# Attention scores of an adaLN layer: rotated q and k transposed once, their high and low rows placed by transfers

## The reference

```
mod = silu(c) @ wmod                      # six rows of 256 a batch: sa ca ga sb cb gb
h   = layernorm(x) * (1 + ca) + sa
q,k,v = h @ Wq + bq, h @ Wk + bk, h @ Wv + bv   # 16 query heads and 4 key/value heads, 16 wide
q,k = rope(q), rope(k)                    # pairs (even, odd) turned by the position's angle
y   = softmax(causal(q k^T / 4)) v        # scores of the four query heads of a key head are summed
x   = x + ga * (y @ Wo + bo)
h   = layernorm(x) * (1 + cb) + sb
x   = x + gb * ffn(h)                     # router, small linear block, rmsnorm, gated 704-wide mlp
```

## Time and profile before

| | |
|---|---|
| median of 3 runs | 486.77 us (486.62 to 486.94) |
| the profiled execution, its own time | 489.17 us |
| its span in the profile | 487.4 us |
| TensorE busy | 444.7 us, 91% |
| VectorE busy | 338.9 us, 70% |
| ScalarE busy | 281.7 us, 58% |
| GpSimd busy | 225.8 us, 46% |

### The profile page before, as it was taken

The page is one execution under the profiler, slowest core; times in us unless marked ns, Lnnn a source line. Parts: engine busy times, 40 slices in busy tenths (PEclk is TensorE's granted clock), DMA queues, the critical chain, the costliest instruction groups (busy, mean ns, idle before and its releaser), DMA issues.

```text
span 487.4 us, 9404 instructions
## 1 busy us (share of the span) xinstructions
PE 444.7 (91%) x3320; PEld 372.3 (76%) x3320; DVE 338.9 (70%) x745; ACT 281.7 (58%) x574; POOL 225.8 (46%) x297
## 2 busy tenths in 40 slices
PE   2687699979999999899999999989999999999994
PEld 2275355677678589778766999879889779999994
DVE  3569968488988337998873688898687635376552
ACT  1183657676559757345487763526857488454440
POOL 5382946621283421331747506275261744348244
PEclk9997989998999999999999999999999999999998
DMA  7904020000000000020020100010001001001011
GB/s 201 300 1 137 2 88 1 1 2 5 3 1 24 1 1 2 1 86 8 3 88 1 34 2 1 5 44 3 1 33 48 1 1 45 1 2 45 1 43 44
DMA packets 16448, 16.04 MB, mean 33 GB/s; under 512 B 4105, under 2 KB 14798, under 8 KB 16402
## 3 DMA queue, kind: packets, MB, share of 16 engines
q1 hardware_dynamic: 16402, 15.43, 10.0%
HBM read 11.09 MB, written 4.21 MB: 31 GB/s over the span
## 4 chain that ended last, share of the span: by engine, by line
PE 80%; DVE 6%; ACT 5%; issue 3%; DMA 2%; SPq 2%; POOL 1%; POOLq 0%; ACTq 0%; DVEq 0%
PE banks L784 8%; PE banks L785 8%; PE banks L786 8%; PE banks L701 8%; PE banks L713 7%; PE banks L675 7%; PE banks L574 5%; PE banks L654 5%; PE banks L575 5%; PE banks L576 5%; PE banks L738 3%; PE banks L664 2%; DMA wm_st<-in_L_wmod 2%; DVE stk L1124 2%; ACT QKT L890 2%
## 5 line engine op out<-in xcount | busy, mean ns | idle before, releaser
L784 PE MATMUL banks<-gTh,guhi 128*128 128x256 f32 x352 | 101.7, 289 | 1.6 <-DVE mx L1139 1.5
L785 PE MATMUL banks<-gTl,guhi 128*128 128x256 f32 x352 | 98.1, 279 | 0.0
L786 PE MATMUL banks<-gTh,gulo 128*128 128x256 f32 x352 | 98.1, 279 | 0.0
L910 ACT ACTIVATE PT<-banks 128x1024 f32<-128x1024 f32 (+3 forms) x96 | 74.4, 809 | 29.0 <-PE banks L701 24.2
L1139 DVE TENSOR_REDUCE mxp<-banks 128x2 f32<-128x1024 f32 (+3 forms) x56 | 62.2, 1142 | 12.1 <-PE banks L675 6.7
L784 PEld LDWEIGHTS banks<-gTh,guhi 128*128 128x128 f32 x352 | 66.5, 189 | 4.2 <-issue 3.5
L785 PEld LDWEIGHTS banks<-gTl,guhi 128*128 128x128 f32 x352 | 66.4, 189 | 0.5
L786 PEld LDWEIGHTS banks<-gTh,gulo 128*128 128x128 f32 x352 | 66.4, 189 | 0.0
L675 PE MATMUL banks<-QKT 128*128 128x512 f32 (+3 forms) x192 | 53.4, 384 | 13.3 <-ACT QKT L890 5.0
L701 PE MATMUL banks<-QKT 128*128 128x512 f32 (+3 forms) x192 | 52.2, 374 | 3.0 <-DMA QKT<-mrT 1.9
L537 POOL TENSOR_SCALAR_AFFINE_SELECT PT<-PT 128x512 f32<-128x512 f32 x32 | 20.7, 647 | 67.6 <-ACT PT L910 67.6
(11 more groups left out here) (165 smaller groups left out, 1069.8 us busy)
## 6 DMA issues: line engine op xcount, KB each, us to landing
xres<-in_L_attn_x SPq DMA_DIRECT2D x8, 512.0 KB, 5.0
out_x<-xres SPq DMA_DIRECT2D x8, 512.0 KB, 3.0
wm_st<-in_L_wmod SPq DMA_DIRECT2D x1, 1024.0 KB, 8.1
modB<-mod_scratch SPq DMA_DIRECT2D x4, 256.0 KB, 3.1
wg_st<-in_L_ffn_w_gate SPq DMA_DIRECT2D x1, 704.0 KB, 5.4
wu_st<-in_L_ffn_w_up SPq DMA_DIRECT2D x1, 704.0 KB, 6.5
xres<-in_L_ffn_w_down SPq DMA_DIRECT2D x1, 640.0 KB, 5.9
wm_st<-in_L_wmod SPq DMA_DIRECT2D x1, 512.0 KB, 4.6
```

The source lines that it names most:

```text
L784: pe.matmul(out_, guhi[:, k, blk, :], gh, start=(m == 0 and k == 0), stop=False)
L785: pe.matmul(out_, guhi[:, k, blk, :], gl, start=False, stop=False)
L786: i = pe.matmul(out_, gulo[:, k, blk, :], gh, start=False, stop=(m == len(blocks) - 1 and k == KB - 1))
L910: act.activation(PT[:, u % 2, 2 * q:2 * q + 2, 0:CH - q0], both("prob", b, n)[:, :, 0:CH - q0], ACT.Exp, scale=float(D) ** -0.5).then_inc( ...
```

## The change

- **Stack.** The buffer `stk` is gone. `stack` transposes `rot` itself: four transposes for a whole chunk (all eight heads of 16 fill 128 columns), two steps a batch, into one bank. `shi` (ScalarE) copies the bank into `qkh`, rounded to the fast format, and `slo` (VectorE) subtracts that from the bank into `qkl`. They take the places of `sthi`, `stlo` and `stk`.
- **Placing.** A new SyncE step `qkd` copies rows of `qkh` and `qkl` into `QKT` by 18 transfers inside SBUF for each chunk: six of 32 rows for q and twelve of 16 rows for k, each row 2 KB. `max` and `prob` wait for all 18 (semaphore `s_qk`) in place of `stk`.
- **Layout.** A pair of heads now takes 96 rows of `QKT` plus 4 for the maxima, with zeros where the other head's key would be. `vkeys` zeroes 96 rows of all four key blocks and writes ones over rows 96 to 99; `mrd` issues two transfers, not four.
- **First loads.** x and the q, k, v weights are issued ahead of the first part of `wmod`; the biases have a semaphore of their own, and `setw` and `asetw` lose their last part to new steps `setb` and `asetb`.
- **Order.** `ORDER` is written anew, for all batches.

```diff
-PE_STEPS = dict(bias=1, xT=NJ, qkv=NJ, stack=NJ, ...
+PE_STEPS = dict(bias=1, xT=NJ, qkv=NJ, stack=NC, ...
+ldx ldx setw stats stats rstd1 norm1 pzero norm1 xT4 vkeys norm1 pmodc vmodc norm1 rstd1 norm1 xT5 asetw asetb pmod
+amod wts xev qkv4 setb bias6 biasq norm1 xT7 xev qkv6 norm1 norm1 xT5 xev qkv7 xev qkv5 qkvb qkvb rope stack6 shi wts
+slo qkvb qkvb rope pprep0 stack5 shi afwv pprep1 aprep aprep aprep aprep gmod gprep gprep gprep ldx slo stats gprep
+awd aw1 gwd rstd1 ldx qkd stats qkd max4 norm1 norm1 norm1 ldx rstd1 mxr max6 norm1 max4 mxr mxr max6 mxr max0 mxr
+max4 mxr mneg ldG ldW max4 max0 max6 max2 mxr mxr mxr mtT0 mrow max6 mxr mxr max4 max2 max0 ldx ldG mrd prob6 mxr max4
...
@@ sync
             for k in range(KB):
                 sp.dma_start(cT[:, k, :], ...).then_inc(l_c, 16)
-            sp.dma_start(wm_st[:, :, 0:CH], ...).then_inc(l_modc, 16)
             load_x(0, 0)
             sp.dma_start(wq_st[:], ...).then_inc(l_qkv, 16)
             ...
+            sp.dma_start(wm_st[:, :, 0:CH], ...).then_inc(l_modc, 16)
...
+                elif kind == "qkd":
+                    wait("shi", n + 1)
+                    wait("slo", n + 1)
+                    if b > 0:
+                        wait("prob", 0)
+                    elif n == 0:
+                        sp.wait_ge(s_keys, 2)
+                    at = slice(n * CH, (n + 1) * CH)
+                    for q in range(2):
+                        for g, part in enumerate((qkh, qkh, qkl)):
+                            sp.dma_start(QKT[g * GR:(g + 1) * GR, q, at].bitcast(F32),
+                                         part[q * GR:(q + 1) * GR, n, :].bitcast(F32)).then_inc(s_qk[n], 16)
+                    for h in range(H):
+                        rows = (H + h) * D
+                        for g, part in enumerate((qkh, qkl, qkh)):
+                            to = g * GR + (h % 2) * D
+                            sp.dma_start(QKT[to:to + D, 2 + h, at].bitcast(F32), part[rows:rows + D, n, :].bitcast(F32)
+                                         ).then_inc(s_qk[n], 16)
@@ tensor
                 elif kind == "stack":
-                    wait("sthi", 2 * n // TPC + 1)
-                    wait("stlo", 2 * n // TPC + 1)
...
-                    for t in range(2):
-                        for q in range(4):
-                            i = pe.transpose(o[:, t, q * P:(q + 1) * P], stk[:, (2 * n + t) % TPC, 2 * q:2 * q + 2, :
-                                             ].rearrange("p h d -> p (h d)"), ident[:])
+                    wait("rope", n + 1)
+                    free(kind, n)
+                    o = of(kind, b, n)
+                    for t in range(TPC):
+                        i = pe.transpose(o[:, t * P:(t + 1) * P], rot[:, t, :, :].rearrange("p h d -> p (h d)"), ident[:])
...
-                    wait("stk", qt // 2 + 1)
+                    pe.wait_ge(s_qk[qt // TPC], QKD * (b + 1))
@@ scalar
-                elif kind == "sthi": ...
-                elif kind == "stk": ...
+                elif kind == "shi":
                     wait("stack", n + 1)
+                    if b > 0:
+                        act.wait_ge(s_qk[n], QKD * b)
+                    act.activation(qkh[:, n, :], of("stack", b, n), ACT.Copy).then_inc(S["shi"], 1)
@@ vector
-                elif kind == "stlo": ...
+                elif kind == "slo":
+                    wait("shi", n + 1)
+                    if b > 0:
+                        dve.wait_ge(s_qk[n], QKD * b)
+                    dve.tensor_tensor(qkl[:, n, :], of("stack", b, n), qkh[:, n, :].bitcast(F32), ALU.subtract
+                                      ).then_inc(S["slo"], 1)
```

More of the change, by code:

```diff
@@ L104 @@
 ORDER = """
[L105 to L109, removed]
@@ L130 @@
-max6 mxr mxr mxr x1 max4 mxr gate0 sil stack6 down0 up3 fin rs1 stk max4 max6 mneg mtT1 mrow fft sum mxr mxr ffhi wo2
-max0 gate4 sil store ldx ldW down5 x1 fft ffhi ffl rstd2 mxr mrd max6 prob2 exp fflo down4 mxr prob0 exp sum max6
-prob2 exp sum max4 a0 pmask mxr mxr rstd2 prob6 prob2 pv1 prob4 stats exp exp exp max6 max2 mxr mxr pmask pv prob4 exp
-pmask pv rstd1 prob6 a4 hT5 bias2 exp pmask pv hhi mneg mtT3 ycopy mrow down6 route ms2 yT3 norm1 norm1 route xT4 ms2
-xev hlo a5 sum ytm ynT3 ynev a4 fin route biasq ms2 mrd prob6 exp prob2 wob wo5 route x1 prob6 prob0 wo4 exp x1 fin
@@ new lines @@
+fft ffhi norm1 rs2 h2 gate3 gate2 sil norm2 hmod h2 ms1 up4 up3 hT1 rope fflo fft stack0 qkd hhi hlo a1 sil h2T4 fft
+shi slo rs1 route ms2 h2hi ffhi ffhi a2 max6 qkd mxr route ms2 max0 max6 h2lo mxr fflo mxr max2 mxr gate4 sil x1 rs2
+h2 h2 gate0 up4 max2 max6 up1 ffl mxr fft mxr sil h2T5 h2hi ffhi fft h2lo down0 sum max6 ffhi ffl mxr fflo max2 gate1
+up0 mxr max6 sil fft mxr gate5 ffhi sil rstd2 norm2 up4 max6 mneg hmod rstd1 max0 fft mxr fflo mxr max2 gate5 sil
+down4 sum mtT5 mrow mrd mxr max6 mxr max0 up5 fft ms1 ffhi ffhi ldB ldW mxr max2 mxr gate4 sil prob6 exp fflo up5 fft
@@ new lines @@
+max0 mxr down2 sum ffl ffhi prob4 exp max6 mxr rs1 pmask prob0 max2 exp max4 prob6 exp pv0 pmask mxr mxr max2 mxr fin
+hT1 hhi prob6 exp down4 prob6 prob2 exp mneg mtT5 mrow mrd fflo wts hlo pv exp pmask prob6 exp xT5 xev norm1 norm1 sum
+pmask fin pv down1 sum pv ycopy wob prob4 exp a1 prob6 prob2 prob4 a0 route route exp exp exp prob6 pv1 prob2 bias0
+yT4 ytm exp biasq ms2 ms2 exp pv prob6 exp xT0 norm1 rs2 norm1 prob2 ynT4 ynev exp prob6 pv exp h2 prob4 wo2 exp h2
+pmask x1 wo3 prob6 pv x1 rstd2 norm2 exp prob4 exp pv h2T2 prob6 h2hi prob4 store ldx h2lo qkv3 pmask rstd2 exp exp
@@ new lines @@
+mxr rstd2 sil h2 h2 gate2 sil max6 fft mxr max4 gate2 ffhi mxr mneg max0 h2T3 hT6 h2hi h2lo hhi sil up7 hlo mxr fft
+max4 mxr gate3 gate6 fflo max0 up7 a4 ffhi ms1 mxr fft ffl rs1 route a5 store sil ldx gate3 up2 ffhi up4 max0 sil
+norm2 fft sil ms2 ffhi route ms2 hmod ms1 fflo down2 max6 rs2 h2 fflo mxr h2 fft ffhi up5 max0 sum ldW mxr mtT4 mrow
+down2 max6 fft mxr mxr max4 hT3 max0 ffhi hhi sum fflo mxr ldG mrd prob6 exp ffl down2 hlo prob4 prob6 exp mxr mneg
+down3 sum fin sum stats wob exp prob6 prob0 exp mtT4 mrow pmask pv2 exp rs1 prob6 prob4 pmask pv exp exp prob0 xT3 exp
@@ L164 @@
+down2 sum sum sum fin fin store store store
 """.split()
@@ L700, in _ @@
                     for e in range(2):
-                        i = pe.matmul(o[:, e, 0:CH - q0], QKT[:, 2 + 2 * q + e, j * P:(j + 1) * P],
-                                      QKT[:, q, c * CH + q0:(c + 1) * CH], start=True, stop=True)
+                        i = pe.matmul(o[:, e, 0:CH - q0], QKT[0:MR + 4, 2 + 2 * q + e, j * P:(j + 1) * P],
+                                      QKT[0:MR + 4, q, c * CH + q0:(c + 1) * CH], start=True, stop=True)
                     i.then_inc(S["prob"], 1)
```

225 lines of the change are left out of this document (97 added, 128 removed).

## The result

The kernel after takes 497.14 us in the median (494.97 to 498.98, 4 runs), the kernel before 486.69 beside it: ratio 1.0187, interval 1.0158 to 1.0216. The ratio is not the quotient of the two medians, which lie 10.5 us apart. The kernel is slower, by about 9 us by the ratio. The forecast said 488.8, slower, and its range ended at 496: the sign came out, the size did not. The profiled execution took 497.03 us with a span of 495.3, so +7.9 in spans where the forecast had +2.0.

A forecast was written before the change was run, and what follows sets the result against it. TensorE was taken as the bound from 75 to 480 us, with batch 0's attention uncovered before. Span 487.4 + 9.8 (mark) - 7.3 (transposes) + 3.2 (later placings) - 3.7 (ended waits) = 489.4, median 488.8; range 480 to 496.

The forecast's parts named there:

- The mark: First probability of batch 0's second chunk, at 74.97 us before; forecast 9.8 us later, with placings at 0.58 an issue.
- Rival C: Issues cost 0.62 us and late waits are renamed, not ended: mark at 86.5, median 496.0 us; chance 0.18.
- The transposes: TensorE in batches 1 to 3: six steps of four transposes for twelve of eight, 7.3 us less.
- Later placings: Batches 1 to 3: TensorE's other work covers the placings except for waits of 3.2 us in sum.
- Ended waits: TensorE's late waits for line 890 (2.7 us) and for reductions (2.3): 3.7 of these 5.0 us taken off.
- Behind the mark together: After the mark: transposes -7.3, later placings +3.2, ended waits -3.7 us.
- the forecast's sign: Listed among what would show the forecast in the changed profile: TensorE busy about 434 us.
- Median and span: Whole kernel: runs' median taken 0.6 us under the profiled span, so 489.4 of span became 488.8.
- A: An issue costs 0.47 us, as loads do: span 483.7, median 483.1 us, faster; chance 0.28.
- B: The first batch is not held up, mark up to 2 us late: median 478.8 us; chance 0.14.

The follow-up runs named there:

- The first experiment: Kernel after with only the six q transfers of each chunk in batch 0, its twelve k transfers left out: 488.18 us, ratio 0.9999 to the kernel before.
- the four-fold experiment: Kernel after with each step of transposes done four times over, 16 instead of 4: 500.92 us, ratio 1.0248 to the kernel before.
- the last experiment: Kernel after with set-up reordered, GpSimd's first weight subtraction held back, and 9 joined transfers a chunk for 18: 485.11 us, ratio 0.9978 to the kernel before.

## Why the prediction came out right in sign and short in size

The mechanism of the first batch was the right one: the price is SyncE's issuing, it is paid in full in batch 0 where nothing covers it, and it outweighs the transposes. The first experiment shows that. Behind the mark a term was missing, TensorE's clock. The terms, in spans:

- **The mark: +9.8 forecast, +12.4 measured.** The start was even better than forecast: `pmod` 19.79 (20.4), the first placing 38.51 (40.1). The mis-sized term is the issue. I took 0.58 from a choice between 0.47 and 0.62; it is 0.63, nearly the spacing of `mrT`, at 32 and at 16 rows. The first chunk also has one issue of 1.69 us among its 18, which take 12.45 us; the second's take 11.45. From the first issue to the second chunk's scores it is 25.4 us for the forecast's 22.0, and the earlier start took back 1.6 of that. So the first scores came at 52.37 (51.7), the second chunk's at 63.96 (62.1). Rival C's 0.62 with its mark at 86.5 was nearest. That is 1.9 of the missing 2.6 us; 0.7 is behind it, 23.4 us from the second landing to the mark for my 22.7.
- **The transposes: -7.3 forecast, 7.2 us of work measured**, by the four-fold experiment, which also shows that some of it stands ahead of waits: there 7.2 us of work moved the stretch behind the mark by 4.8 (406.1 for 401.3). By estimate it is up to 8.9 us of work, with that run's clock counted.
- **Later placings: +3.2 forecast, 2.6 of idle time measured.** That was about right. Without two thirds of their transfers 5.6 us went in all, and the rest is no wait: it goes with the clock. In the kernel after TensorE comes out of its wait of 2.44 us at half its clock, 0.60 granted from 222.5 to 226.4 us, where the earlier trace rows has 1.00 for the stretch as a whole. In the kernel with a third of batch 0's transfers it comes out of the same wait at 1.00. So the wait alone doesn't set it.

```profile
222.50:226.40 3.90, 3.88 (x21) 3.10 (x21) 2.28 (x3) 1.72 (x6) 0.00 (x0) 0.60 0.45 101
```

- **Ended waits: -3.7 forecast.** TensorE's idle time behind the mark went from 12.5 to 11.1 with 3.3 us of new DMA waits in it. So the idle time of other causes fell by 4.7, and that although the removed transposes may have filled waits (2.4 us of idle time went when as many were added). The forecast's 3.7 was, if anything, too small. The order was written anew at the same time, and no run separates what it ended from what the shorter chains of ScalarE and VectorE ended.
- **Behind the mark together: -7.8 forecast, -4.5 measured.** TensorE's busy time fell by 3.1, not by 7.2, and over the whole span it is 441.9 where the forecast's sign was 434. Half-clock stretches behind the mark grew by 6.8 us, which is worth half of that, 3.4; 0.7 us is left unexplained (2.4 with 8.9 us for the transposes). The sum had no term for this, and what sets the place of such a stretch these runs leave open. The page "TensorE: Matmul & The Clock Gate" of the Trainium skill, in "Part 4: PE-mode transpose", says that a transpose does not count as work for the clock as a matmul does. These runs can't show it either way: behind 20 transposes in the wait the granted clock was 1.00 from 222.4 to 226.4 us, as behind 40 matmuls, but it was 1.00 behind the empty wait of 2.45 us too. In both experiments the stretch at 339 us went as well, in one of them with nothing put there.
- **Median and span.** I took the median 0.6 below the span of the profiled run. The changed kernel's median lies 1.8 above its span. The profiled run of before, 489.17, was 2.4 above its median; that of after, 497.03, was at its median. So of the 8.3 us by which 488.8 missed, 5.9 are in the spans and 2.4 in this offset.

Rivals A and B fall by the same rows, 0.63 us from one transfer to the next: A needed 0.54 or less, and B a first batch that isn't held up, where the mark came 12.4 us later. Rival C's 496.0 came nearest to the median, and in part by luck: its price of an issue held, but it had nothing for ended waits, where idle time of other causes fell by 4.7, and the clock's 3.4 us, for which it had no term either, stand in for much of that.

The Trainium skill's advice to join transfers under 64 KB ("DMA: Bandwidth & Descriptors", "Rules for kernel authors") is borne out by the last experiment, where 9 transfers of twice the size do the work of 18 at half the issuing time. The same page of the Trainium skill, in "Issuing engines are not separate DMA queues", says that the time to initiate a DMA is usually small relative to the DMA itself. It is not in a row of such transfers: the first chunk's 18 issues take 12.45 us, and TensorE is released 1.4 us after the last.

## What to carry to other kernels

Count the transfers, not their bytes, when rows are placed inside SBUF: each held the queue that issued it for 0.63 us here, at 16 rows, at 32, and at rows of two pieces, and where the consumer has nothing else to do (the first batch here) the whole row of issues is on the path. Lay the source out so that one transfer serves several destinations along the free dimension; the fastest kernel here has that, at the price of two extra instructions a chunk. When an order is remade, look at what GpSimd and VectorE now do at the same time: over five microseconds went there twice without any wait in the profile. And where TensorE bounds a stretch, count how long it was granted half its clock before a change of busy time is put down to an edit.

## What the runs showed of the hardware that was not expected

- **VectorE held off by GpSimd.** A 128x256 subtraction of VectorE took 6.41 us, and two 128x192 scalings 5.73, while GpSimd ran 640-wide subtractions without a gap; with GpSimd held back they took 0.42 and 0.63. The kernel before has such a row too, beside GpSimd's subtractions from 36.55 to 39.78 us: 3.24 us, where others of its shape take 0.41 to 0.48. In the profile this looks like busy time, not like a wait. The Trainium skill, "SBUF — State Buffer", section "SBUF: two separate sides", says that the two engines lock a shared pair of ports for whole instructions. The rows agree, and show more: the loser sat out several GpSimd instructions in a row, since each took 0.9 us and the delay was 6.

```profile
36.38 3.24 DVE L1124 TENSOR_TENSOR stk<-qk,cos_t 128x256 f32<-128x256 f32 x1 [0.99 <-PE banks L664]
```

- **ScalarE's issuing** costs as much as SyncE's, 0.61 to 0.62 us each, and single ones more, beside SyncE's at the same time (2.84 us for two at 227.92).
- **Half the rows, the same time.** Copies and subtractions out of PSUM took 0.59 and 0.69 us at 64 rows as at 128.
